# Last stage of a four-block network: the choice of experts in two halves of tokens, the end of the second half between the weighings

## The reference, cut to what matters

```python
def _L3_ffn_ref(x, router_w, router_b, expert_w, expert_b):
    B, N, D, C, E, K = (8, 2048, 32, 32, 8, 2)
    router_probs = jax.nn.softmax(x @ router_w + router_b, axis=-1)
    top_p, top_i = jax.lax.top_k(router_probs, K)
    top_p = top_p / jnp.sum(top_p, axis=-1, keepdims=True)
    expert_out = jnp.einsum('bnd,edc->bnec', x, expert_w) + expert_b
    gathered = jnp.take_along_axis(expert_out, top_i[..., None], axis=2)
    return jnp.einsum('bnk,bnkc->bnc', top_p, gathered)
...
    t = _to_tokens(x)
    t = t + _L3_ffn_ref(_ln_t(t), L3_ffn_router_w, L3_ffn_router_b, L3_ffn_expert_w, L3_ffn_expert_b)
```

## Time and profile before

| what | value |
| --- | --- |
| median of three runs | 560.86 us (560.37 to 563.21) |
| the profiled execution, its own time | 561.55 us |
| its span in the profile | 559.1 us |
| mean granted TensorE clock | 0.886 of full speed |
| busy over the span: PE, DVE, ACT, POOL | 432.0, 370.2, 236.3, 226.9 us |
| last stage: first instruction of the choice | 483.44 us |
| last stage: first weighing | 500.56 us |
| last stage: end of the last sum into the residual | 555.23 us |

### The profile page before, as it was taken

How to read it: one execution, slowest core, us unless ns; L and a number is a source line. 1 busy time by engine, 2 the same in 40 slices (tenths; PEclk the granted TensorE clock), 3 DMA queues, 4 the chain that set the end, 5 groups by cost and what they waited for, 6 DMA issues and landing times.

```text
span 559.1 us, 8700 instructions
## 1 busy us (share of the span) xinstructions
PE 432.0 (77%) x3066; PEld 329.5 (59%) x3066; DVE 370.2 (66%) x1228; ACT 236.3 (42%) x569; POOL 226.9 (41%) x293
## 2 busy tenths in 40 slices
PE   2788868986897757995589976799589848809996
PEld 2456744663347634994389964498355737606664
DVE  4988597749795696007924477501978498398885
ACT  1497555412774554673510024476379634000000
POOL 2598185004582491000500005000359278029994
PEclk9999999678998998899569997799589996558999
DMA  8300000000000000000000000000000000001223
GB/s 162 79 2 1 1 1 1 1 2 0 1 1 1 2 0 1 1 1 2 0 2 2 1 1 1 1 1 1 2 0 2 1 1 1 1 0 20 38 40 56
DMA packets 34670, 6.03 MB, mean 11 GB/s; under 512 B 33713, under 2 KB 34369, under 8 KB 34626
## 3 DMA queue, kind: packets, MB, share of 16 engines
q1 hardware_dynamic: 34626, 5.46, 5.6%
HBM read 3.36 MB, written 2.10 MB: 10 GB/s over the span
## 4 chain that ended last, share of the span: by engine, by line
PE 48%; DVE 37%; ACT 5%; POOL 5%; issue 2%; DMA 1%; SPq 1%; DVEq 0%; POOLq 0%
PE psum L1360 7%; DVE moments L330 6%; DVE ab L742 6%; PE psum L1122 5%; PE psum L1121 5%; DVE ab L726 4%; PE psum L616 4%; PE psum L461 4%; PE psum L1533 3%; POOL z L392 2%; PE psum L627 2%; PE psum L586 2%; PE psum L1553 2%; PE psum L1538 2%; POOL gate L804 2%
## 5 line engine op out<-in xcount | busy, mean ns | idle before, releaser
L461 PE MATMUL psum<-ident,z 128*128 128x128 f32 x256 | 54.2, 354 | 34.5 <-POOL z L392 31.4
L461 PEld LDWEIGHTS psum<-ident,z 128*128 128x128 f32 x256 | 38.5, 182 | 61.9 <-POOL z L392 43.2
L586 PE MATMUL psum<-wp_L,z_t 64*128 64x320 f32 x384 | 66.1, 473 | 3.4 <-ACT z_t L370 2.1
L330 DVE BATCH_NORM_STATS2 moments<-x_cols 128x6 f32<-128x64 f32 x448 | 61.6, 211 | 0.3
L392 POOL TENSOR_TENSOR z<-z,stats 128x496 f32<-128x496 f32 (+1 forms) x35 | 36.8, 1052 | 58.6 <-DVE z L316 58.6
L370 ACT ACTIVATE z_t<-psum 128x512 f32<-128x512 f32 x56 | 40.0, 719 | 33.5 <-PE psum L461 33.4
L586 PEld LDWEIGHTS psum<-wp_L,z_t 64*128 64x128 f32 x384 | 33.2, 192 | 31.0 <-issue 27.6
L387 POOL MEMSET z<- 128x16 f32 x32 | 4.0, 126 | 112.2 <-DVE z L316 111.8
L1213 ACT ACTIVATE ab<-psum,mv 128x128 f32<-128x128 f32 x108 | 39.7, 368 | 19.0 <-PE psum L1122 8.9
L392 POOL TENSOR_TENSOR z<-x_cols,stats 128x512 f32<-128x512 f32 x21 | 22.0, 1048 | 62.9 <-DVE stats L336 62.5
L1122 PE MATMUL psum<-ab,R_vt 128*128 128x128 f32 x216 | 46.8, 300 | 0.0
(11 more groups left out here) (256 smaller groups left out, 912.9 us busy)
## 6 DMA issues: line engine op xcount, KB each, us to landing
x_cols<-in_x_dram SPq DMA_DIRECT2D x16, 128.0 KB, 2.8
out_dram<-x_cols SPq DMA_DIRECT2D x32, 64.0 KB, 1.9
par<-in_par_dram SPq DMA_DIRECT2D x1, 644.5 KB
w<-in_w_dram SPq DMA_DIRECT2D x4, 64.0 KB, 2.3
w<-in_w_dram SPq DMA_DIRECT2D x1, 256.0 KB, 2.7
mask<-in_mask_dram SPq DMA_DIRECT2D x1, 64.0 KB, 2.8
row<-in_row_dram SPq DMA_DIRECT2D x1, 3.3 KB
w_bias<-in_w_dram SPq DMA_DIRECT2D x1, 8.0 KB, 1.9
```

The costliest lines, as they stand in the source:

```text
L330: m = dve.bn_stats(moments[:, q, k:k + 2, :].rearrange("p k m -> p (k m)"), X4[:, SQ * q + s, g:g + 2, :].rearrange("p g c -> p c g"))
L461: m = pe.transpose(bank(b % 2)[:, k * N:(k + 1) * N], block_of(Z)(4 * b + k), ident[:, :])
L586: m = pe.matmul(bank(slot_bank(s) + h, 2 * 5 * C), ZT[rows, s, :], wp[l][rows, :, :], start=True, stop=True)
```

## The change

The choice is made in two halves of 64 tokens for each partition, that is of the steps 0 to 15 and 16 to 31. PE raises `rt_ps` once more, after the fourth group of logits. DVE does the whole choice of the first half, then that of the second half up to the difference of its two largest logits. The rest of the second half, six instructions, is put between the weighings of the first six pairs: after steps 2, 4, 8 and 10. ACT and POOL do their parts once for each half. `F3_LOGITS_READ`, the count of `top` after which PE may write over the logits, is raised to the second half's last reading of them.

```diff
-        F3_LOGITS_READ = 6
+        F3_LOGITS_READ = 13 + 6
...
                 if b >= 3:
-                    route(b - 1)
+                    m = route(b - 1)
+                if b == 4:
+                    m.then_inc(L.s["rt_ps"], 1)
...
-            act.wait_ge(L.s["diff"], L.at["diff"] + 1)
-            act.activation(W1S, DIF, ACT.Sigmoid).then_inc(L.s["sg"], 1)
-            act.activation(W2S, DIF, ACT.Sigmoid, scale=-1.0).then_inc(L.s["sg"], 1)
+            for a in range(2):
+                half = slice(a * N // 2, (a + 1) * N // 2)
+                act.wait_ge(L.s["diff"], L.at["diff"] + a + 1)
+                act.activation(W1S[:, half], DIF[:, half], ACT.Sigmoid).then_inc(L.s["sg"], 1)
+                act.activation(W2S[:, half], DIF[:, half], ACT.Sigmoid, scale=-1.0).then_inc(L.s["sg"], 1)
...
+            def rank_best(logits, m, r, a):
+
+                then(dve.tensor_tensor(tokens(r, a), tokens(logits, a), per_token(m, a), ALU.is_equal))
+                then(dve.tensor_tensor(tokens(r, a), tokens(r, a), ranks, ALU.mult))
+
+            def mark_best(rm, hot, r, a):
+
+                then(dve.tensor_reduce(tokens(rm, a), tokens(r, a), AX.X, ALU.max))
+                then(dve.tensor_tensor(tokens(hot, a), tokens(r, a), per_token(rm, a), ALU.is_equal))
+
+            def first_choice(a):
+                dve.wait_ge(L.s["rt_ps"], L.at["rt_ps"] + a + 1)
+                then(dve.tensor_reduce(tokens(M1, a), tokens(LOGITS, a), AX.X, ALU.max))
+                rank_best(LOGITS, M1, RANK1, a)
+                mark_best(R1M, RT[1], RANK1, a)
+                then(dve.scalar_tensor_tensor(out=tokens(RT[2], a), in0=tokens(RT[1], a), scalar=-FAR,
+                                              in1=tokens(LOGITS, a), op0=ALU.mult, op1=ALU.add))
+                then(dve.tensor_reduce(tokens(M2, a), tokens(RT[2], a), AX.X, ALU.max))
+                dve.tensor_tensor(tokens(DIF, a), tokens(M1, a), tokens(M2, a), ALU.subtract).then_inc(L.s["diff"], 1)
+
+            def second_weight(a):
+                dve.wait_ge(L.s["sg"], L.at["sg"] + 2 * a + 2)
+                then(dve.tensor_tensor(tokens(RT[3], a), tokens(RT[3], a), per_token(W2S, a), ALU.mult))
+
+            def both_weights(a):
+                dve.wait_ge(L.s["hot"], L.at["hot"] + a + 1)
+                then(dve.tensor_tensor(tokens(RT[4], a), tokens(RT[5], a), tokens(RT[3], a), ALU.add))
+
+            first_choice(0)
+            rank_best(RT[2], M2, RANK2, 0)
+            mark_best(R2M, RT[3], RANK2, 0)
+            second_weight(0)
+            both_weights(0)
+            first_choice(1)
...
             for j in range(EPAIRS):
                 weigh(2 * j)
+                if j == 1:
+                    rank_best(RT[2], M2, RANK2, 1)
+                if j == 2:
+                    mark_best(R2M, RT[3], RANK2, 1)
+                if j == 4:
+                    second_weight(1)
+                if j == 5:
+                    both_weights(1)
                 weigh(2 * j + 1)
...
-            pool.tensor_tensor(RT[5], RT[1], W1S.unsqueeze(2).to_broadcast([N, N, E3]), ALU.mult).then_inc(L.s["hot"], 1)
+            for a in range(2):
+                half = slice(a * N // 2, (a + 1) * N // 2)
+                pool.wait_ge(L.s["sg"], L.at["sg"] + 2 * a + 1)
+                pool.tensor_tensor(RT[5][:, half], RT[1][:, half], W1S[:, half].unsqueeze(2).to_broadcast([N, N // 2, E3]),
+                                   ALU.mult).then_inc(L.s["hot"], 1)
```

More of the change, by code:

```diff
@@ L1582, in then @@
                 dve.wait_ge(sm, n[0])
-            def per_e(t):
-                return t.unsqueeze(2).to_broadcast([N, N, E3])
-            ranks = rank[:, :].unsqueeze(1).to_broadcast([N, N, E3])
             dve.wait_ge(L.s["rank"], L.at["rank"] + E3)
[L1589 to L1607, removed]
+            def tokens(t, a):
+                return t[:, a * N // 2:(a + 1) * N // 2]
@@ new lines, in per_token @@
+            def per_token(t, a):
+                return tokens(t, a).unsqueeze(2).to_broadcast([N, N // 2, E3])
+            ranks = rank[:, :].unsqueeze(1).to_broadcast([N, N // 2, E3])
+            def rank_best(logits, m, r, a):
[4 more added lines that the diff above has]
+                then(dve.tensor_tensor(tokens(hot, a), tokens(r, a), per_token(rm, a), ALU.is_equal))
@@ L1648, in f3_pool @@
             L = f3
-            pool.wait_ge(L.s["sg"], L.at["sg"] + 1)
-            pool.tensor_tensor(RT[5], RT[1], W1S.unsqueeze(2).to_broadcast([N, N, E3]), ALU.mult).then_inc(L.s["hot"], 1)
+            for a in range(2):
[3 more added lines that the diff above has]
+                                   ALU.mult).then_inc(L.s["hot"], 1)
             for s in range(S - 1):
```

## The result

The changed kernel takes 553.62 us (median of 4 runs, 551.70 to 554.87) against 560.62 us of the kernel before (4 runs, 559.12 to 563.21): a ratio of **0.987**, 95% interval 0.982 to 0.992. Two later sets of six runs, each beside runs of the kernel before, gave 551.82 (ratio 0.985, 0.981 to 0.988) and 553.07 (0.985, 0.983 to 0.988). The forecast was 552.3.

The account below looks back on a forecast made before the run. DVE alone moves the program for 17.12 us up to the first weighing, then PE sets the pace. First weighing 10.7 earlier less 2.05 for put-back work is 8.65; against 560.86 that gives 552.3 us, range 551.0 to 555.8.

Parts of the forecast that it names:

- Where the gain is: Last stage: first weighing 10.7 us earlier, 2.05 lost to put-back work, 8.65 us gained in sum.
- The rival that the first half doesn't start early: First half of the choice let go only at 483.44: 560.6 us, no change; chance 0.04.
- Price of halves: DVE's choice on 512 elements: 0.725 us an instruction with the step to the next, 0.455 the product, 0.15 the difference.
- First weighing: Start of the first weighing on DVE: at 489.85 instead of 500.56, 10.7 us earlier.
- first half's product "meets POOL": First half of the choice: DVE's product ends 0.27 us behind POOL's; without the wait, 0.8 us earlier.
- What is put back: Six DVE instructions, 4.08 us, among the weighings of steps 2 to 11: stretch to step 12 longer by 2.05 us.
- the lock: DVE instructions with two SBUF operands wait for POOL's current one: about 0.55 us behind step 2, 0.1 behind steps 4 and 10.
- The clock: PE's granted clock in the last stage: 1.00 (2.4 GHz) from about 497, wrong if below 1.00 beyond 500.
- a late rise: Rival, PE's clock rises later: each late pair costs 2.6 us, one or two pairs, about 556 us; chance 0.08.
- POOL and the lock: Rival among the weighings: two to three extra POOL instructions of 1.25 us, gain 5.0 to 7.0, about 554.9; chance 0.14.
- the 491 that was named: Sign at the first weighing: the forecast is wrong, in the price of halves, if it comes later than 491.
- The clock's limit of 500: Sign in the last stage: the forecast is wrong if PE's granted clock is below 1.00 beyond 500.

Follow-up runs that it names:

- square of kernels: Kernel before, changed kernel, e1_early, e2_between and e3_split: early start and interleaving taken apart; stages 81.62, 72.29, 74.82, 81.49 and 84.05 us.
- e2_between: Changed kernel, but the first half also waits for all logits; interleaving kept: 560.53 us, ratio 0.9985 to the kernel before.
- e3_split: Changed kernel with neither early start nor interleaving, only the choice in two halves: 563.92 us, ratio 1.003 to the kernel before.
- e1_early: Changed kernel with the early start, but all of the second half ahead of the first weighing: 553.47 us, ratio 0.985 to the kernel before.
- e5_poolsum: Changed kernel with the sum of the first half's two weights moved from DVE to POOL: 552.64 us, ratio 0.985 to the kernel before.
- e6_smallpool: Changed kernel with POOL's half and quarter sums cut to 4 of 128 columns: stage 71.72 us, its one run 553.16 us.
- e4_warm: Changed kernel with PE computing the experts of step 0 three times more before the first weighing: 552.58 us, ratio 0.982 to the kernel before.
- after_again: The changed kernel unchanged, run and profiled a second time: 551.82 us, ratio 0.985 to the kernel before, stage 73.23 us.
- e8_fill: Changed kernel with extra early expert passes on PE and unread products behind the experts of steps 1, 4 and 6: 551.38 us, ratio 0.984 to the kernel before.

## Why the prediction came out right, step by step

*Where the gain is.* Right. The square of kernels gives 9.2 for the early start and 2.5 for the interleaving, less 2.4 for the halves: 9.3, where the prediction had 8.65. The rival that the first half doesn't start early falls with the reduction at 477.96; e2_between is that rival built, and measures no change, as the rival said.

*Price of halves.* Right: reductions, marks and the masking took 0.69, 0.72 with the step to the next, the product 0.42, the difference 0.22 with its successor 0.14 to 0.16 behind. e3_split puts the cost of the halves at 2.43 us, where all its work is ahead of the weighings.

*First weighing.* Forecast 16.24 behind the start of L349, measured 15.38, so 11.57 earlier instead of 10.7. The term that was mis-sized is the **first half's product "meets POOL"**: 0.8 us were put down for it, and it took its bare 0.42, at 483.61. The working took POOL's start as 0.57 behind the difference; it was 1.25 (483.99 - 482.74), since the sigmoid that releases POOL stands on ACT behind the last copy of the turned input (L370, 483.17, 0.60), which was not there when the difference came at 491.70 before. POOL then met the one-hot mark instead, for 0.14. The remaining 0.2 of the 0.86 are small steps, such as the start 1.30 instead of 1.4 behind L349. The edit was costed at DVE and POOL, and ACT's queue, past which the sigmoids were moved, was called idle. Where the difference comes with no copy on ACT, the sum's own rule is seen. e2_between's first half, the same instructions begun 8.5 us later, has POOL's product 0.59 behind the difference, and DVE's product is held to 1.18 (first row). So it is in e1_early's second half, with the difference at 487.80 (order of time, POOL and DVE).

```profile
488.21 1.18 DVE L1602 TENSOR_TENSOR ranks<-ranks,rank 128x512 bf16<-128x512 bf16 x1
```

```profile
488.39 1.17 POOL L1681 TENSOR_TENSOR ab<-ab,squares 128x512 f32<-128x512 f32 x1 [7.42 <-ACT squares L1574]
...
488.67 1.18 DVE L1602 TENSOR_TENSOR ranks<-ranks,rank 128x512 bf16<-128x512 bf16 x1
```

*What is put back.* Forecast 2.05 lost, measured 2.08 in the first profile. The parts differ a little: the lock took 1.04 where about 0.75 was put down (0.53 behind step 2 against 0.55, 0.25 and 0.26 behind steps 4 and 10 against 0.1 each, none behind step 8, as said); waiting for PE, and for a place that POOL frees, took 0.23 and 0.25. That makes 1.52 where 0.95 was put down. The stretch still came out since DVE's own work was put about 0.6 too high: rows that follow each other overlap (497.45 + 2.36 = 499.81, and the next starts at 499.73), which the working did not take off. So the nearness of 2.08 to 2.05 is luck. The marks wait as well, L1601 and L1607, which no row of before showed. The Trainium skill, page "SBUF — State Buffer", section "Who interferes with whom", says that a DVE instruction with two SBUF inputs contends with a GpSimd one that reads SBUF, and a reduction does not. This trace agrees: both marks read two SBUF tensors, and the reduction between them (L1606) took its bare 0.68 beside POOL's sums.

*The clock.* Half right. The forecast had 1.00 from about 497 and called a late rise a rival of 0.08. The late rise came in both repeats of the changed kernel, and in e5_poolsum and e6_smallpool; in e4_warm the clock rose and fell back. But its price was not the 2.6 that the rival gave for a pair: one group of experts and one sum ran at the low level while DVE had work of its own, and 0.94 remained. With it the stage is 8.39 shorter than before, without it 9.33; the forecast of 8.65 lies between. That it lies so near to 8.39 is luck: the first weighing gained 0.86 more than forecast, the late clock took 0.94, and POOL's tail, below, 0.16.

*POOL and the lock.* No weighing from step 12 on waited for POOL, and the lock took 1.04 us, not the two to three instructions of 1.25 of the rival, so the rival falls. POOL's way from its first half sum to the end of its last grew from 50.2 to 52.3 us, by less than the five times 0.55 that the prediction allowed. The tail's half sum gave 0.23 to it, and from step 12 to its end the stage takes 35.98 us, where it took 35.82.

*What would have made it wrong.* The first weighing came at 492.04, past the 491 that was named; that limit was a time of the wall, and the stage started 3.05 later. Counted from L349 the limit is 17.4 and the weighing came at 15.38. Such limits should be set from a mark next to the change. The clock's limit of 500, 26.4 behind L349, was nearly reached by after_again: the clock was 0.72 in 499 to 501, 25 to 27 behind, and the sum that PE began at 500.10, 26.0 behind, took its fast 0.62.

*From the stage to the total.* The stage's 9.33 or 8.39 stands beside 7.0, 8.6 and 7.6 between the medians of three sets. In the profiles L349 starts between 472.57 and 476.66. The granted clock scatters there too, on code that the change does not touch: from 420 to 470 us it was 0.95 before and 0.90 in the first profile after, from 60 to 120 us 0.89 and 0.85. Whether this is what moves the start was not tested.

## What to carry to other kernels

Split work that waits for a whole tensor when the first half of its input lies there long before: here 8.5 us of waiting were worth 9.2 against 2.4 of fixed cost for the added instructions. Before pricing a step that moves forward, write down what stands ahead of each of its parts on every engine that it touches, the small ones too: at its new place a different neighbour is running. Judge a change of one stage by that stage, counted from an instruction just ahead of it, since two microseconds of scatter elsewhere can hide or invent the gain.

## What was not expected of the hardware

The clock of TensorE is not a function of the program alone: the same instructions after nearly the same gap ran step 5 of the experts in 1.13 us in one profile and in 2.08 us in two others. Gaps that another engine makes can take it back as well: in e4_warm it was 1.00 in 492 to 494 and 0.53 in the next 2 us, with PE busy 1.57 and 1.51 of 2; in e8_fill, with the gaps partly filled, it stayed at 1.00 through stretches with 0.37 and 0.94 of 2 us busy, and in e2_between, with nothing filled, through one with 0.53. What decides between these was not settled.

POOL's product of 128x512 with one factor spread over the experts took 1.07 us (1.17 where it met DVE's product), its sum of two full tensors of that size 1.26 to 1.27; the estimate had 1.27 for both, half of the 2.54 in the earlier trace rows. The kernel before has the same two times elsewhere: its product L804, whose factor is spread over neighbouring columns as here, takes 1.05 us on the mean of 24, its sum L719 1.28. A spread factor alone does not make it short: L710, whose factor is a row of values repeated as a whole, takes 1.28 too. Why L1650 took 2.54 was not tested.
